# Attention's buffers laid out anew in on-chip memory, the first chunk of the second feed-forward layer rewritten with tanh, and three long pieces cut into parts

## What is computed

```python
def ffn(x):                       # weights in {-1, 0, 1}; 704 hidden columns
    g = (x @ gate_w.T) * gate_s
    u = (x @ up_w.T) * up_s
    return ((silu(g) * u) @ down_w.T) * down_s

x = x + 0.5 * ffn(layernorm(x))
x = x + attention(layernorm(x))   # 16 heads of 16, rotary q and k, causal softmax, output projection
x = x + 0.5 * ffn(layernorm(x))
```

## Time and profile before

| what | us |
|---|---|
| median of three runs | 862.66 (862.34 to 863.26) |
| the profiled execution | 865.6 |
| its span, from the first to the last instruction | 863.6 |
| PE busy | 823.4 |
| DVE busy | 614.7 |
| ACT busy | 548.5 |
| POOL busy | 391.6 |

### The profile page before, as it was taken

How to read it: one execution, slowest core, us unless ns; L and a number is a source line. 1 busy time by engine, 2 the same in 40 slices (tenths; PEclk the granted TensorE clock), 3 DMA queues, 4 the chain that set the end, 5 groups by cost and what they waited for, 6 DMA issues and landing times.

```text
span 863.6 us, 17536 instructions
## 1 busy us (share of the span) xinstructions
PE 823.4 (95%) x6400; PEld 561.6 (65%) x6400; DVE 614.7 (71%) x1257; ACT 548.5 (64%) x1064; POOL 391.6 (45%) x428
## 2 busy tenths in 40 slices
PE   6999999998999999999999999999999989999996
PEld 5788887776655555655555565555555447987885
DVE  5566568694998898878888878888979604554542
ACT  3666664544657867666867747677667986655642
POOL 2768785547043363360362542331233325665553
PEclk8999999998999999999999999999999999999998
DMA  9800323104584474552454734553551110010001
GB/s 315 309 2 30 113 69 119 39 3 84 155 230 136 96 187 125 163 147 82 108 133 149 186 76 139 115 115 83 164 125 42 41 52 26 25 49 25 25 25 50
DMA packets 65794, 89.78 MB, mean 104 GB/s; under 512 B 19756, under 2 KB 31404, under 8 KB 65452
## 3 DMA queue, kind: packets, MB, share of 16 engines
q1 hardware_dynamic: 65564, 88.57, 37.1%
q10 hardware_dynamic: 144, 0.07, 0.0%
HBM read 45.52 MB, written 40.76 MB: 100 GB/s over the span
## 4 chain that ended last, share of the span: by engine, by line
PE 73%; DVE 13%; ACT 9%; issue 2%; POOL 2%; DMA 1%; SPq 1%; DVEq 0%; POOLq 0%; ACTq 0%
PE psum L872 15%; PE psum L977 13%; PE psum L935 10%; PE psum L841 10%; PE psum L898 9%; PE psum L960 9%; DVE NP L1196 4%; ACT PT L1083 3%; DVE SH L1196 3%; PE psum L851 3%; PE psum L945 2%; PE psum L858 2%; ACT XN L1018 2%; DVE ST L1111 1%; ACT G_f L1037 1%
## 5 line engine op out<-in xcount | busy, mean ns | idle before, releaser
L1083 ACT ACTIVATE PT<-psum 128x512 f32<-128x512 f32 (+2 forms) x640 | 306.7, 585 | 131.4 <-PE psum L960 131.0
L1196 DVE TENSOR_REDUCE NP<-psum 128x1 f32<-128x512 f32 (+2 forms) x448 | 260.3, 643 | 31.1 <-PE psum L945 22.0
L1299 POOL TENSOR_SCALAR_AFFINE_SELECT PT<-PT 128x512 f32<-128x512 f32 x128 | 80.5, 636 | 217.6 <-ACT PT L1083 217.5
L960 PE MATMUL psum<-Q,K 50*128 50x512 f32 (+2 forms) x768 | 147.2, 411 | 10.8 <-ACT PT L1083 7.9
L935 PE MATMUL psum<-K,Q 48*128 48x512 f32 (+2 forms) x768 | 146.8, 408 | 4.2 <-DVE SH L1196 1.3
L872 PE MATMUL psum<-XH,WG_f 128*128 128x512 f32 x352 | 144.3, 410 | 5.2 <-DVE HF_f L1147 3.7
L977 PE MATMUL psum<-PT,V 128*32 128x512 f32 (+3 forms) x1536 | 145.2, 496 | 0.2 <-ACT PT L1083 0.2
L872 PE MATMUL psum<-XL,WG_f 128*128 128x512 f32 x352 | 139.9, 397 | 0.0
L1256 POOL TENSOR_TENSOR HL_f<-HF_f,HH_f 128x512 fp32r<-128x512 f32 x80 | 102.6, 1292 | 72.4 <-ACT HH_f L1047 72.3
L1147 DVE SCALAR_TENSOR_TENSOR HF_f<-psum,US,G_f 128x512 f32<-128x512 f32 x96 | 71.2, 749 | 73.4 <-PE psum L872 32.5
L1196 DVE TENSOR_REDUCE SH<-psum 128x2 f32<-128x256 f32 (+2 forms) x192 | 102.5, 590 | 16.2 <-PE psum L945 15.3
(11 more groups left out here) (78 smaller groups left out, 1106.4 us busy)
## 6 DMA issues: line engine op xcount, KB each, us to landing
zd<-ZH SPq DMA_DIRECT2D x32, 512.0 KB, 4.9
Q<-zd SPq DMA_DIRECT2D x64, 192.0 KB, 4.0
K<-zd SPq DMA_DIRECT2D x64, 192.0 KB, 5.1
zd<-ZL SPq DMA_DIRECT2D x16, 512.0 KB, 4.9
od<-OS SPq DMA_DIRECT2D x32, 256.0 KB, 3.4
OC<-od SPq DMA_DIRECT2D x32, 128.0 KB, 2.7
SC<-rd_ SPq DMA_DIRECT2D x32, 128.0 KB, 2.9
out<-X SPq DMA_DIRECT2D x16, 256.0 KB, 2.1
```

Source lines behind the costliest of these rows:

```text
L960: ins = tn.matmul(dst, K[k][r, p, j * P:(j + 1) * P], Q[k][r, p, 512 * c2 + base:512 * c2 + 512], start=True, stop=True)
L1083: sc.activation(dst, src, ACT.Exp, scale=0.25).then_inc(S["act_exp"], 1)
L1196: ve.tensor_reduce(out=acc, in_=src, axis=AX, op=ALU.max, negate=True).then_inc(S["dve_max"], 1)
L1299: gp_.affine_select(out=pt, in_=pt, compare_op=ALU.is_ge, fill=0.0, base=0, pattern=[[0, 4], [1, P]], channel_multiplier=-1).then_inc(S["p ...
```

## The change

**Layout.** `zone` now begins with PT, V1, OS, OC and SC, then Q and K of pair 2; pair 1 lies behind FFN 1's 70,656 bytes. Everything but pair 1 still lies over FFN 1's bytes and still waits for its end; pair 1, used by group 1 first, waits for nothing of FFN 1. FFN 2's small tiles move from pair 0 to the place behind its weights, and its rows over pairs 2 and 1. Its first small tiles wait for `dma_w2` alone.

**Tanh.** Chunk 0 of FFN 2 computes silu as (tanh(g s / 2) + 1) g times a scale that is folded into up's (two small POOL instructions, `pool_gh`, make GSH and UG). ACT's instruction becomes a tanh, DVE gets one more instruction per i, which reads the gate's PSUM bank, and the bank stays taken until then. The silu pieces of chunk 1 wait for the last exponentials instead of those of chunk 0. Chunks 0 and 1 of FFN 2 get their `x_pass` 30 places ahead instead of 11.

**Pieces.** The bn_stats become four pieces of their own, `act_xn` four, and `dve_rope` two.

**Numbers of the scheduler.** MODE_PLACE 1.112 to 1.513, WINDOW 52.283 to 57.161, AHEAD 4.439 to 4.045, WARM_SHARE 0.567 to 0.523.

```diff
+def by_tanh(ph, c, i):
+    return ph == 2 and c in BY_TANH
...
-MODE_PLACE, WAIT_NS, DMA_RATE, WINDOW = 1.112, 80, 200.0, 52.283
+MODE_PLACE, WAIT_NS, DMA_RATE, WINDOW = 1.513, 80, 200.0, 57.161
...
-AHEAD = 4.439
-WARM_SPAN, WARM_SHARE, WARM_COLD = 2700.0, 0.567, 10000.0
+EARLY = 30
+BY_TANH = (0,)
+AHEAD = 4.045
+WARM_SPAN, WARM_SHARE, WARM_COLD = 2700.0, 0.523, 10000.0
...
-        add(at + 2, 4 * 491, "act_xn", who, c, after=[("pool_rs", who, c)] + ([("pe_xT",) + xn + (1,)] if xn else []))
+        for i in range(4):
+            add(at + 2, 491, "act_xn", who, c, i, after=[("pool_rs", who, c)] + ([("pe_xT",) + xn + (1,)] if xn else []))
...
-            first = [("pe_st", GROUPS - 1, 1, 7, "a")] + [("act_exp", GROUPS - 1, 1, 7, "a", hh) for hh in range(2)] if ph == 2 and c == 0 else []
+            turned = by_tanh(ph, c, i)
+            first = [("act_exp", GROUPS - 1, 1, 7, "a", hh) for hh in range(2)] if ph == 2 and c <= len(BY_TANH) and not turned else []
...
-                add(key(2 * w + 1), 4 * dve_ns(512), "dve_rope", b, cc, w, after=banks_of + free + [("dma_cos",), ("dma_sin",)], empties=banks_of)
+                for ab in range(2):
+                    add(key(2 * w + 1), 2 * dve_ns(512), "dve_rope", b, cc, w, ab, after=banks_of[ab:ab + 1] + free + [("dma_cos",), ("dma_sin",)],
+                        empties=banks_of[ab:ab + 1])
...
-        add(A[0] - 5, 1200, f"dma_on{k}", after=split if k == 0 else ffn1_end)
+        add(A[0] - 5, 1200, f"dma_on{k}", after=(split, [("pool_const",)], ffn1_end)[k])
...
-            room = [("pe_st", gr - QK, 1, 7, "a")] if gr >= QK else split if gr == 0 else ffn1_end
+            room = [("pe_st", gr - QK, 1, 7, "a")] if gr >= QK else (split, [], ffn1_end)[gr]
...
-    passes += [(f2[c] - 11, lambda c=c: x_pass("f2", c, f2[c] - 11)) for c in range(8)]
+    early = [f2[c] - (EARLY if c < 2 else 11) for c in range(8)]
+    passes += [(early[c], lambda c=c: x_pass("f2", c, early[c])) for c in range(8)]
...
-        at = zone
-        for k in (1, 2):
-            qks, at = lay(at, (f"Q{k}", [P, 2, T], F32R), (f"K{k}", [P, 2, T], F32R))
-            Q.append(qks[0])
-            K.append(qks[1])
-        PT, at = lay(at, *((f"PT{i}", [P, 2048], F32) for i in range(PTN)))
+        PT, at = lay(zone, *((f"PT{i}", [P, 2048], F32) for i in range(PTN)))
...
+        qk2 = at
+        (Q2, K2), at = lay(qk2, ("Q2", [P, 2, T], F32R), ("K2", [P, 2, T], F32R))
+        at = max(at, zone + FFN1_BYTES)
+        (Q1, K1), at = lay(at, ("Q1", [P, 2, T], F32R), ("K1", [P, 2, T], F32R))
...
-        for ph, spots in ((1, (zone, None, None)), (2, (w2, qk0, zone))):
+        for ph, spots in ((1, (zone, None, None)), (2, (w2, None, qk2))):
...
+                    turned = by_tanh(ph, c, i)
+                    if turned:
+                        e.wait_ge("pool_gh")
+                    sc.activation(G[ph][slot[f"Gf{ph}", a]][gl if turned else ul, :], bank(*gate)[gl, :], ACT.Tanh if turned else ACT.Silu,
+                                  scale=(GSH if turned else GS)[gl, i:i + 1]).then_inc(S["act_silu"], 1)
...
+                    if turned:
+                        gate = ("pe_g" if i < NI - 1 else "pe_u",) + a
+                        gl = h_lanes(i)[0]
+                        e.wait_ge(*gate)
+                        e.wait_ge("pool_gh")
+                        ve.scalar_tensor_tensor(G[ph][k][ul, :], G[ph][k][gl, :], 1.0, bank(*gate)[gl, :], ALU.add, ALU.mult).then_inc(S["dve_ha"], 1)
+                        e.wait_ge("dve_ha", *a)
+                    ve.scalar_tensor_tensor(HF[ph][k][ul, :], bank("pe_u", *a)[ul, :], (UG if turned else US)[ul, i:i + 1], G[ph][k][ul, :],
                                             ALU.mult, ALU.mult).then_inc(S["dve_h"], 1)
```

More of the change, by code:

```diff
@@ L33 @@
 QK, PTN, HSLOTS = 3, 3, 8
+FFN1_BYTES = 70656
 TURN_POOL = ()
@@ L69, in raises @@
             some = some[1:]
+        if kind == "dve_h" and not by_tanh(*a):
+            some = ()
         return [(s, 1) for s in some] + [(kind, 1)]
@@ L378, in x_pass @@
         st, xn, x = p.prior["ST", (who, c)], p.prior["XN", (who, c)], p.prior["XA" if (who, c // 2) == ("a", 0) else "X", (who, c)]
[L379 removed]
+        ready = x_ready(who, c)
+        for i in range(4):
+            add(at, 350, "dve_bn", who, c, i, after=[ready[i // 2 if len(ready) > 1 else 0]] + ([("act_xn",) + st + (3,)] if st else []))
+        add(at, 350, "dve_va", who, c, after=[("dve_bn", who, c, i) for i in range(4)])
         add(at, 1400, "pool_rs", who, c, after=[("dve_va", who, c)])
[L381 removed]
+        for i in range(4):
+            add(at + 2, 491, "act_xn", who, c, i, after=[("pool_rs", who, c)] + ([("pe_xT",) + xn + (1,)] if xn else []))
         for kt in range(2):
[L383 removed]
+            add(at + 4, 400, "pe_xT", who, c, kt, after=[("act_xn", who, c, i) for i in range(4)] + [("act_id",)] + (x_users(*x) if x else []), room=(1,))
             add(at + 5, act_ns(512), "act_xh", who, c, kt, after=[("pe_xT", who, c, kt)] + (x_users(*x) if x else []))
@@ L406, in consts @@
         add(-10, 2600, "pool_v1", 0)
+        add(f1[3], 400, "pool_gh", after=[("dma_gs",), ("dma_us",)])
     def ffn(ph, c, at):
@@ L426, in ffn @@
             gate = ("pe_g" if i < NI - 1 else "pe_u", ph, c, i)
[L427 to L430, removed]
+            add(key + 1, 586, "act_silu", ph, c, i, after=[gate] + ([("dve_h",) + g] if g else []) + first + ([("pool_gh",)] if turned else []),
+                empties=[gate] if i < NI - 1 and not turned else [])
+            add(key + 2, 1500 if turned else 774, "dve_h", ph, c, i, after=[("act_silu", ph, c, i), ("pe_u", ph, c, i)] + ([hl_by(*g)] if g else []),
+                empties=[("pe_u", ph, c, i)] + [gate] * (turned and i < NI - 1))
             add(key + 2, 550, "act_hh", ph, c, i, after=[("dve_h", ph, c, i)] + room)
@@ L658, in macaron @@
         US = place("US", [P, NI])
+        GSH = place("GSH", [P, NI])
+        UG = place("UG", [P, NI])
         EB = place("EB", [P, 2, P], BF16)
@@ L854, in tensor_program @@
                     e.wait_ge("act_id")
-                    e.wait_ge("act_xn", who, c)
+                    for i in range(4):
+                        e.wait_ge("act_xn", who, c, i)
                     take(piece)
@@ L1010, in scalar_program @@
                 elif kind == "act_xn":
-                    who, c = a
+                    who, c, i = a
                     k = slot["ST", (who, c)]
@@ L1016, in scalar_program @@
                         e.wait_ge("pe_xT", *was, 1)
[L1017 to L1020, removed]
+                    sc.activation(XN[:, i, :], X[:, tile_of(who, c, i), :], ACT.Identity,
+                                  bias=NB[k][:, i:i + 1], scale=RS[k][:, i:i + 1]).then_inc(S["act_xn"], 1)
                 elif kind == "act_xh":
@@ L1035, in scalar_program @@
                     elif ph == 2:
-                        e.wait_ge("pe_st", GROUPS - 1, 1, 7, "a")
-                    sc.activation(G[ph][slot[f"Gf{ph}", a]][ul, :], bank(*gate)[gl, :], ACT.Silu, scale=GS[gl, i:i + 1]).then_inc(S["act_silu"], 1)
+                        e.wait_ge("dma_w2")
+                    turned = by_tanh(ph, c, i)
[3 more added lines that the diff above has]
+                                  scale=(GSH if turned else GS)[gl, i:i + 1]).then_inc(S["act_silu"], 1)
                 elif kind == "act_hh":
@@ L1101, in vector_program @@
                 kind, a = piece[0], piece[1:]
-                if kind == "dve_va":
+                if kind == "dve_bn":
+                    who, c, i = a
+                    k = slot["ST", (who, c)]
+                    was = prior["ST", (who, c)]
+                    ready = x_ready(who, c)
+                    e.wait_ge(*ready[i // 2 if len(ready) > 1 else 0])
+                    if was:
+                        e.wait_ge("act_xn", *was, 3)
+                    ve.bn_stats(ST[k][:, i, :], X[:, tile_of(who, c, i), :]).then_inc(S["dve_bn"], 1)
+                elif kind == "dve_va":
                     who, c = a
                     k = slot["ST", a]
[L1105 to L1109, removed]
                     for i in range(4):
-                        ins = ve.bn_stats(ST[k][:, i, :], X[:, tile_of(who, c, i), :])
-                    ins.then_inc(S["dve_bn"], 1)
-                    e.wait_ge("dve_bn", *a)
+                        e.wait_ge("dve_bn", who, c, i)
                     for i in range(4):
```

45 lines of the change are left out of this document (27 added, 18 removed).

## The result

| | before | after |
|---|---|---|
| median us | 862.5 (859.5 to 863.3) | 836.96 (833.5 to 838.8) |
| profiled span | 863.6 | 836.8 |
| first exponential | 204.2 | 204.5 |
| end of the last group's maxima, about | 680.5 | 662.9 |
| end of the last exponential | 713.3 | 701.5 |

The ratio is 0.9711, 95% interval 0.9686 to 0.9736: 24.9 us faster at 862, where 14.0 was forecast. The profiled execution of the kernel before took 865.6 us, some 3 us over its median, so differences from its trace come out that much too large in sum.

A forecast was written before the change was run, and what follows sets the result against it. It took PE as nearly full, with a third lost in two short stages and attention bound by a mixture of PE and DVE. Tail 8.5 plus middle 5.5 made 14.0, giving 848.7 us from the median 862.66; range 840 to 862.

The forecast's parts named there:

- The pieces and the numbers: Cutting bn_stats, scaled rows and rotation, plus new scheduler numbers: set to 0, bounds -1.5 and 2 us.
- The middle: Between FFN 1 and attention: group 1's maxima fill the gap before the first exponential; gain 5.5 us, bounds 10.7 and 0.
- The tail: Chunk 0 of FFN 2 runs beside group 15's exponentials; gain 8.5 us, bounds 12.3 and 1.7.
- every sign that I had named for the tail: Tanh between exponentials, no table load, ACT above 92%, fillers under 3 us, stage 37 to 41, FFN 2 some 14 shorter.
- The stretch: How much longer group 15's stage gets with chunk 0 beside it: 5.8 us, with ACT's share at 0.95.
- rival 2: Tail: chunk 0 displaces exponentials one for one, ACT keeps 88%, stretch 9.1, tail gain 1.7 to 4; 854 us, chance 0.12.
- the down product not done in time: Tail: a third of chunk 0's down product, 1.8 us, taken off as not done by the last exponential.
- Tanh's table: Tail: tanh shares exp's table set by the Trainium skill, so tanh among exponentials costs no load.
- Rival 4: Tail: tanh has its own table, up to twelve loads, 15.4 to 25 us; 864 to 874 us, chance 0.05.
- Rival 1: Attention: the heads set its pace, so the maxima moved ahead gain only 0 to 1; 854 us, chance 0.15.
- Rival 3: Tail: the order keeps chunk 0 behind the heads or its banks come too late, gain 0; 857 us, chance 0.06.
- Rival 5: Tail: chunk 0's banks choke the scores, ACT stands once per piece, losing 12.8 us; 861.5 us or slower, chance 0.10.

The follow-up runs named there:

- c1: The kernel before with only the new layout and pair 1 free of FFN 1; no pieces, no tanh, numbers and x passes as before: 856.42 us.
- a3: The changed kernel with pair 1's loads and ones waiting for the end of FFN 1 as before: 848.69 us.
- a2_no_tanh: The changed kernel with silu instead of tanh for chunk 0 of FFN 2, after the last exponential: 838.60 us.
- b2: The kernel before with only statistics, scaled rows and rotation cut into pieces; layout, silu and numbers as before: 845.80 us.
- b3: The kernel before with statistics, scaled rows and rotation cut into pieces, and the changed kernel's scheduler numbers: 846.91 us.
- b4: The kernel before with only the scaled rows cut into four pieces: 858.52 us.
- b6: The kernel before with statistics and scaled rows cut, the rotation in one piece: 846.73 us.
- b5: The kernel before with only the rotation cut in two: 864.91 us.
- a13: The changed kernel with the scheduler's four numbers of before and without tanh: 846.38 us.

## Why the prediction was wrong, by its steps

- **The pieces and the numbers, set to 0 with bounds -1.5 and 2: this step failed.** The cuts are worth 17.9 us on the kernel before and 21.6 in the changed one, the numbers up to 7.5. I bounded them by PE's idle time in FFN 1, "4.0 us to give in all". The bound was the wrong kind. PE's 132.04 us in 50 to 186 hold 19.23 of projections and 9.09 of maxima, attention's work, which could as well come later; FFN 1 became 7.1 and 8.2 us shorter with the cuts. And it looked at FFN 1 alone, where attention gave 8.2 and 4.9 and FFN 2 3.1. The chain's lines for XN and ST (2% and 1% of it) and the wait of bn_stats for XN stood in the trace of before, and I did not read them. The lower end of the range also left out this step's own bound of 2 us; with it the range would begin at 837.7, still above 836.96.
- **The middle, 5.5 us: right in size for the layout alone, not in its working.** The layout alone gives 4.7 (2.1 to 7.4), though with the x passes and on top of the pieces it gave -1.6 or 7.1, by the scheduler's numbers. DVE's gap of 9.96 us is gone, and 34 of group 1's 48 maxima matmuls, 71%, are in before 204 us, where I had reckoned 55%. But attention shrank by 14.4 us in c1, as by the 14.5 of DVE that I set aside for PE's 7.9, and most of it was given back: 3.9 in FFN 1, and 5.6 between the last row maximum and the last exponential, since the heads did not keep up. That these come out near 5.5 is partly luck. The first exponential did not move (204.5), as said, but as the sum of two: without the head start, in a3, it comes at 194.9. The granted clock in 204 to 212 is back in c1_layout_only:

```profile
204.00:208.00 4.00, 3.82 (x28) 2.46 (x24) 4.00 (x9) 3.85 (x9) 1.66 (x3) 1.00 0.85 199
208.00:212.00 4.00, 4.00 (x36) 2.27 (x34) 3.96 (x13) 3.32 (x7) 4.00 (x5) 1.00 1.00 203
```

  It was 0.50 and 0.72, after PE had stood for 3.11 us; here PE has no such gap. The changed kernel has 1.00 there too, but 0.77 and 0.81 in 188 to 196 us, where PE is busy for 2.42 of the first 4.
- **The tail, 8.5 us: right as a difference of the two traces, wrong as a cause.** Before and after give 15 us less behind the last exponential and some 6 more ahead of it, 9.2, and every sign that I had named for the tail but ACT's share came. But a2_no_tanh has most of that already: its stage is 29.10 where before's from 680.5 was 32.8, and what follows 147.8 where it was 150.3, 6.2 us in all. Tanh's own share is 1 to 3. Two terms were mis-sized. The stretch is 9.5 us, where I took 5.8: ACT's share is 34.20 / 38.60 = 0.89, as the earlier trace rows had it (0.88), not the 0.95 I took. So rival 2 was the right reading of the stage. And for the down product not done in time I took off a third, 1.8, where 28 of 44 matmuls, 3.4, were left. The other runs show who brought the 6.2. Behind the last exponential the kernels before with cut scaled rows (b2, b3, b4, b6) have 146.0 to 147.2 us, the others (c1, b5) 149.9 and 149.7. The shorter stage comes with the numbers: 28.7 from the last row maximum in b3 and 28.4 in a2, against 32.4 in b2 and 32.3 in a13. The earlier place of the x passes, which b2, b3 and b6 don't have, is not needed for either.
- **Tanh's table.** The four table loads of before are still four. A tanh stands between exponentials with no load about it, as the Trainium skill says in "ScalarE: Activation LUTs", section "Table sets: the hidden batching unit". The six take 742 ns in the mean where silu took 682. The three behind idle time took 0.68 to 0.69 us, as a silu; the three that start while an exponential still runs show 0.76 to 0.82, overlap included:

```profile
669.11 0.45 ACT L1108 ACTIVATE PT<-psum 128x256 f32<-128x256 f32 x1
669.37 0.76 ACT L1061 ACTIVATE G_f<-psum,GSH 128x512 f32<-128x512 f32 x1
```

  Rival 4 falls.
- **Rival 1, that attention's pace isn't set by maxima**, is not shown, but part of it is seen: in c1 the last row maximum comes 14.4 us sooner (666.8 for 681.2) and the last exponential only 8.8, fillers are still 25.63 us in attention, and with the old numbers the layout added nothing to the pieces. Rival 3 falls: chunk 0 lies in the tail. Rival 5 did not come: in the tail ACT waits for scores once, for 0.46 us.
- **The sum.** 5.5 for the middle and 1 to 3 for tanh would have been 6.5 to 8.5; the rest of the 24.9 is the pieces, and the numbers with the new layout. The total was not only short: more than half of it was for a reason that does not hold at its size.

## What to carry to other kernels

Where an order is fixed per engine, a long piece can cost not its own time but that of everything queued behind it, on every engine that takes part; cutting it is to be priced by the chain that ends the stage, not by the idle time of the busiest engine, which may be busy with work that isn't due. A difference of two traces over a stage does not name its cause: undo the part and look again. And before single edits are compared under a list scheduler, shift its numbers once, to know how far apart two arbitrary orders lie.

## What was not expected of the hardware

Nothing in the engines' durations. But orders of the same instructions, set by four numbers of the scheduler alone, gave 837.0, 843.7 and 845.7 us, a spread of 1%, and the middle setting was the slowest.
